# Rows of an image 34 words apart in place of 33

## What is computed

```
x = x + lattice(gn(x))        # 4 x 4 cells; each: concat of 1..3 inputs, 3x3 conv, bias, relu, 16..48 outputs
x = x + circular_conv(gn(x))  # 3x3, wraps around the edges (given as an FFT product)
x = x + spline_conv(gn(x))    # 3x3 over silu(x) and 8 cubic B-spline bases of x
x = x + conv(gn(x))           # 3x3, zero padding, bias
```

## Time and profile before

| | us |
|---|---|
| median of the runs | 1327.87 |
| lowest and highest of three | 1321.79, 1328.02 |
| span of the profiled execution, first to last instruction | 1313.7 |
| TensorE matmuls busy in it | 1177.5 |
| TensorE weight loads busy | 874.4 |
| VectorE busy | 772.7 |
| ScalarE busy | 701.6 |

### The profile page before, as it was taken

How to read it: one execution, slowest core, us unless ns; L and a number is a source line. 1 busy time by engine, 2 the same in 40 slices (tenths; PEclk the granted TensorE clock), 3 DMA queues, 4 the chain that set the end, 5 groups by cost and what they waited for, 6 DMA issues and landing times.

```text
span 1313.7 us, 14883 instructions
## 1 busy us (share of the span) xinstructions
PE 1177.5 (90%) x5088; PEld 874.4 (67%) x5088; DVE 772.7 (59%) x946; ACT 701.6 (53%) x740; POOL 380.5 (29%) x570
## 2 busy tenths in 40 slices
PE   1378998979999999999999999999998957999995
PEld 1255576756666677776666677777777745777774
DVE  6478983157555532235655553236656579889962
ACT  2456774254544444435454443333445499899931
POOL 7623333244531102122122213523034431102002
PEclk9989999989999999999999999999999978899997
DMA  7589998899999967889999987878789214676684
GB/s 98 148 210 236 258 269 226 203 196 205 211 209 187 215 175 200 226 185 193 219 205 181 206 235 190 244 199 218 188 206 170 45 25 68 100 117 102 108 127 62
DMA packets 108751, 232.12 MB, mean 177 GB/s; under 512 B 41332, under 2 KB 55236, under 8 KB 100484
## 3 DMA queue, kind: packets, MB, share of 16 engines
q1 hardware_dynamic: 91552, 205.02, 69.3%
q0 software_dynamic: 16576, 25.89, 10.6%
q10 hardware_dynamic: 548, 0.27, 0.2%
HBM read 122.05 MB, written 85.75 MB: 158 GB/s over the span
## 4 chain that ended last, share of the span: by engine, by line
PE 51%; SPq 17%; issue 7%; DVE 6%; ACT 6%; DMA 3%; POOL 1%; DVEq 0%; ACTq 0%; POOLq 0%
PE PB L1660 43%; SPq L762 13%; PE PB L1631 7%; SPq L745 4%; DMA lattice<-S 1%; DVE F L1486 1%; DVE S L1499 1%; ACT S L1184 1%; ACT F L1099 1%; PE PB L1622 1%; ACT F L1209 1%; DVE S L1493 1%; DMA S<-lattice 1%; ACT KAN L1082 1%; DMA F<-F 1%
## 5 line engine op out<-in xcount | busy, mean ns | idle before, releaser
L1660 PE MATMUL PB<-F,WA 128*96 128x512 f32 (+1 forms) x3792 | 920.9, 404 | 53.6 <-DVE F L1411 34.5
L1660 PEld LDWEIGHTS PB<-F,WA 128*96 128x96 f32 (+1 forms) x3792 | 664.7, 176 | 300.7 <-issue 52.3
L1099 ACT ACTIVATE F<-S 128x2116 fp32r<-128x2116 f32 (+4 forms) x160 | 261.4, 1635 | 228.5 <-issue 110.6
L1110 ACT ACTIVATE S<-PB,BIAS 96x512 f32<-96x512 f32 (+1 forms) x320 | 210.2, 680 | 276.0 <-PE PB L1660 275.8
L1399 DVE TENSOR_TENSOR F<-S,F 128x1089 fp32r<-128x1089 f32 (+2 forms) x80 | 121.4, 1518 | 198.9 <-ACT F L1099 198.6
L1411 DVE CAST F<-F 64x528 fp32r<-64x528 f32 (+4 forms) x304 | 190.7, 676 | 3.5
L1401 DVE TENSOR_TENSOR F<-S,F 128x1058 fp32r<-128x1058 f32 x64 | 80.7, 1261 | 183.1 <-ACT F L1099 182.5
L1631 PE MATMUL PB<-F,WA 128*128 128x512 f32 x576 | 150.7, 421 | 22.4 <-DVE F L1486 22.4
L854 POOL DMA_DIRECT2D WA<-taps x84 | 61.4, 735 | 350.4 <-ACT S L1110 335.7
L1631 PEld LDWEIGHTS PB<-F,WA 128*128 128x128 f32 x576 | 115.0, 201 | 52.6 <-issue 23.9
L1402 DVE TENSOR_TENSOR F<-S,F 64x1058 fp32r<-64x1058 f32 x64 | 79.9, 1248 | 0.0
(11 more groups left out here) (123 smaller groups left out, 746.8 us busy)
## 6 DMA issues: line engine op xcount, KB each, us to landing
lattice<-S SPq DMA_DIRECT2D x48, 817.5 KB, 6.0
S<-lattice SPq DMA_DIRECT2D x448, 66.1 KB, 4.7
lattice<-S SPq DMA_DIRECT2D x96, 272.5 KB, 3.9
S<-lattice SPq DMA_DIRECT2D x160, 136.1 KB, 2.9
S<-lattice SPq DMA_DIRECT2D x72, 272.5 KB, 4.9
S<-lattice SPq DMA_DIRECT2D x160, 70.1 KB, 2.9
S<-lattice SPq DMA_DIRECT2D x80, 136.2 KB, 4.6
S<-lattice SPq DMA_DIRECT2D x160, 66.0 KB, 2.8
```

The costliest lines, as they stand in the source:

```text
L1099: act.activation(piece_view(s, h, 0), raw_view(s, h), ACT.Copy).then_inc(hi_ready, 1)
L1110: act.activation(wide(to[:, at:at + TS])[:, :, 0:RX], pixels(RING_BANK[n % SLOTS_O][0:cell.rows, :]), ACT.Relu, bias=BIAS[0:cell.rows, k:k ...
L1660: last = nc.tensor.matmul(bank, WA[0:rows, first:first + cell.rows], wide(FZ[0:rows, i % SLOTS_F, base:base + TS])[:, :, 0:RX], start=j == ...
```

## The change

`RW` becomes `RX` + 2 = 34. With it `TS` is 544, `EVEN` 578, `PATCH` 1122, `SEG` 1123, `LEAD` 545, `PIECE` 2246 words. The longer buffers take more memory; the output buffer is cut into two tensors, and the one for odd images lies where the tap buffers RAW and RAW_ONE lay, now parts of one tensor TAPS_IN.

```diff
-RW = RX + 1
+RW = RX + 2
 TS = RQ * RW
...
-        RAW = [sb(f"RAW{i}", [NG * C, NG * C * 9]) for i in range(2)]
-        RAW_ONE = [sb(f"RAW_ONE{i}", [C, C * 9]) for i in range(2)]
+        TAPS_IN = sb("TAPS_IN", [4 * C, 2 * NG * C * 9 + 2 * C * 9])
+        RAW = [TAPS_IN[0:NG * C, i * NG * C * 9:(i + 1) * NG * C * 9] for i in range(2)]
+        RAW_ONE = [TAPS_IN[0:C, 2 * NG * C * 9 + i * C * 9:2 * NG * C * 9 + (i + 1) * C * 9] for i in range(2)]
         KAN = sb("KAN", [P, FEATS * K3, KC])
-        OT = sb("OT", [4 * C, 2, RQ, WD])
+        OT_NEW = sb("OT_NEW", [4 * C, RQ, WD])
+        OT = [OT_NEW[:, :, :], TAPS_IN[:, 0:RQ * WD].rearrange("p (y w) -> p y w", w=WD)]
...
-                yield out[b].rearrange("c (q r) w -> r c q w", r=4)[y], OT[y * C:(y + 1) * C, b % 2]
+                yield out[b].rearrange("c (q r) w -> r c q w", r=4)[y], OT[b % 2][y * C:(y + 1) * C]
...
-                        OT[:, b % 2].rearrange("p y (w s) -> p s y w", s=2)[:, s],
+                        OT[b % 2].rearrange("p y (w s) -> p s y w", s=2)[:, s],
```

## The result

The changed kernel takes 1346.47 us (median of four runs, 1342.11 to 1348.47), the kernel before 1327.94 beside it (1321.79 to 1332.1). The ratio of the two is 1.0171, with a 95% interval of 1.0135 to 1.0206: **slower by 1.7%**. The two medians lie 18.5 us apart, 1.4%, which is near the lower end of that interval; 1.71% of before would be 22.7 us. The time is outside the predicted range (1312 to 1337), on the side that had 0.17. The profiled execution took 1345.35 us, 1.85 more than its span of 1343.5.

What follows compares the result with a forecast made beforehand. It took TensorE's lattice matmuls to bound the middle and ScalarE the spline stage. Span 1313.7 - 4.8 (matmuls) + 3.5 (spline) + 2.0 (early transfers) = 1314.4 us, plus 14.2 outside the span: 1328.6 us, range 1312 to 1337.

Steps and rivals of the forecast that it cites:

- What bounds the kernel: Middle, 285 to 853 us: TensorE is busy throughout at full clock, so the lattice matmul's cost sets the time.
- That a matmul's fetch costs beyond its columns: Lattice matmuls at full clock: 24.4 ns of each 237.7 ns go to fetching the moving operand, not the array's columns.
- The price of a row: Lattice matmuls: 2.03 ns per row off a multiple of four words, so pitch 34 saves 4.8 us in all.
- The spline stage: Spline stage, going at ScalarE's pace: feature operations on 3% more words add 3.5 us (2 to 5).
- The part before 250 us: Start of the lattice, where SP has no slack: 3% more bytes in transfers add 2 us (0 to 4.5).
- Shared memory at nothing: Output buffer laid over the tap buffers: costs nothing, since the taps' last reader comes before its first write.
- Odd rows alone: Rival for matmul reads: only rows starting at odd words cost, 14.4 us saved, 1319.0 us; chance 0.30.
- even starts free: Rival for matmul reads: even starts lose their surplus, odd ones cost as now, about 1283 us; chance 0.10.
- The hop costs, whatever the start: Rival for matmul reads: they stay at 237.7 ns, longer operations add 5.5 us, 1333.4 us; chance 0.26.
- The base: Whole kernel: the profiled span of 1313.7 us lies 14.2 us below the median run, added to reach the forecast.

Runs made afterwards that it cites:

- experiment 4: Changed kernel with its large matmuls reading at pitch 32, all else at 34; 1324.82 us, ratio 0.9999. Its count: time over 0.24 us between starts over 0.3 us apart.
- experiments 5: TensorE alone, output zeros: 16 rows of 32 words, pitches 33 to 66, from words 0 to 3; pitch 41 from word 0 about 250 ns a matmul.
- experiment 9: TensorE alone, output zeros: 32 rows of 16 words, pitches 16 to 24, from words 0 to 3; pitch 20 from words 1 to 3 costs 40 to 43 ns over word 0.
- experiment 8: Changed kernel with all large matmuls reading at 33 and the spline's feature operations on 528 words; 1329.14 us, ratio 1.0059.
- experiment 7: Changed kernel with only the lattice's matmuls reading at 33, the spline's and last convolution's at 34; 1332.53 us, ratio 1.0084.
- experiment 2: Changed kernel with rows back at 33 words, keeping the shared memory; 1324.6 us against 1324.03, ratio 1.0013.
- experiments 1: TensorE alone, output zeros: 40 matmuls of each of 39 read patterns, twice; from word 0, pitch 33 takes 234.9 ns and 34 takes 246.8.

## Why the prediction was wrong

**What bounds the kernel: right.** TensorE fills the middle at the full clock, and the middle follows the matmul: 3088 matmuls of cells 5 to 15 by the 5.8 ns of the lattice's means are 17.9 us. The middle grew by 17.0 us from the one trace to the other; over all traces it is 776.7 us in the mean where the reads are at 33 and 790.7 at 34, 14 us. The rest is about what the waits get shorter: by the count of experiment 4 they come to 15.8 us in the mean at 33, and to 12.3 and 9.8 in the two traces at 34.

**That a matmul's fetch costs beyond its columns: right in kind, too large.** Of the 24.4 ns over 512 columns, contiguous rows from word 0, alone, keep 13.7 (227 against 213.3). At most some 10 ns come from the pitch of 33 and the starts; in the kernel, reading at 32 in place of 33 gives back 4.6.

**The step that failed is "The price of a row":** the 2.03 ns for "a row that is off a group of four words", each row counted by itself and priced by where it starts. By it pitch 34 was to save 2.9 ns in each matmul of kind "33", 4.8 us in all. The runs show the other sign. In the kernel, matmuls of every kind take more at 34, from any start: 5.8 ns in the mean (243.7 against 237.9). Alone, 33 takes 233.4 to 237.4 ns and 34 takes 240.0 to 246.8 over the four starts. And the kernel before with nothing but the lattice's reads at 34 is 1.24% slower. So 14 to 17 us were to be lost in the middle where 4.8 were to be gained. The mixture of starts in the trace before, which the prediction itself notes, couldn't show this.

Why a gap of two words is dearer than a gap of one word is argued and not shown. The account that comes nearest counts the groups of four over the whole matmul. At pitch 33 a row's last words and the next row's first can lie in one group, so that the 527 words from first to last are 132 groups (133 from words 2 and 3), not the 140 of the count by rows; at 34 the 542 words are 136 (137 from word 3), whether rows share groups, as from odd words, or not, as from even ones. The change then adds 3 to 4 groups from any start, which fits the alike starts, and 5.8 ns would be some 1.5 to 1.9 for each, near the 2.03 taken. But the patterns of experiments 5 and 9 that this count has wrong, and the length of the jump as a rival, leave it a guess.

The Trainium skill's "SBUF — State Buffer" (Specifications), with its penalty for each new 16-byte line, agrees in kind with the dearer reads of pitch 20 from words 1 to 3 (1.3 to 1.9 ns for each further group); the 42, 50 and 22 from odd words and the 66 differ from it, and the measurement decides. The even-word rule of the Trainium skill's "Vector Engine (DVE) Microarchitecture Reference" (§5.2) didn't carry over: at pitch 34, starts at 0, 1, 2 and 3 cost the same within 2 ns in the kernel.

**The spline stage: right.** The three kernels with 528-word tiles and experiment 8 take 223.3 to 225.4 us from the spline on (mean 224.8), the four with 544 words 227.9 to 229.6 (mean 228.7): 3.9 us for the predicted 3.5. By the stage's time, experiment 8 shows that the feature operations are its cause, experiment 7 that the matmuls aren't.

**The part before 250 us: right place, under-sized.** Cells 0 to 4 take 212.8 to 214.9 us with 33-word data (mean 213.8) and 217.0 to 219.7 with 34 (mean 218.3), whatever the matmuls read at: 4.5 us, where 2 were taken and 4.5 was the upper bound. The DMA share of the stretch is 0.99 (0.97 in the earlier trace rows), and SP's groups of five, now

```profile
124.52 6.07 SPq L764 DMA_DIRECT2D S<-lattice  x5
...
154.91 4.63 SPq L764 DMA_DIRECT2D S<-lattice  x5
160.25 4.93 SPq L764 DMA_DIRECT2D S<-lattice  x5
```

take 5.03 us in the mean of the seven between 100 and 165 us, where the eight before took 4.94: 1.7% more, no more than the bytes grew. Bytes fit, but no run parted them from the longer splits and from images that begin at odd words, so the cause is argued. The first matmul starts 3 us later on average with 34-word data (55.9 to 60.3 against 54.0 to 56.2); that overlaps, and stays open.

**Shared memory at nothing: right** (experiment 2).

**The rivals.** Odd rows alone, and even starts free, needed a difference by start that isn't there. "The hop costs, whatever the start" ended nearest, on the slower side, and its longer operations are in the result, with 8.4 us (4.5 and 3.9) for its 5.5; but it left matmuls at 237.7 ns, and they went to 244.

**The base.** Of the 14.2 us added between span and median about 1.8 lie around the span; the rest was that the execution profiled was faster than the four runs beside it. This shifts no sign.

## What to carry to other kernels

Padding that looks better aligned can be dearer: here rows 34 words apart cost more than rows 33 apart, from every start. Where a trace holds only one mixture of patterns, as this one did, a loop of matmuls alone prices the pitch, and is worth more than a share worked out of the mixture. Price the very shape that the kernel reads: the count of groups over the whole matmul had the sign right for 16 rows of 32 words, but with eight rows of 64 a gap of one word was no cheaper than two, and other pitches broke the count. And a bound taken away shows the next one: at pitch 32 the matmul lost 4.6 ns, and waits took back most of it.

## What was not expected of the hardware

Contiguous rows from word 0, alone and at the full clock, start 227 ns apart and not 213; the runs don't say why. One contiguous row of 512 words costs 9.7 ns more from word 1 than from word 0, for a single further group; from word 3, with the same further group, it is 2 ns (pitch 16 of experiment 9, 228.9). A gap of one whole group costs about 6 ns a matmul, whether there are 15 gaps (pitch 36 from word 0, 233.5; 236.7 in experiment 9) or 3 (four rows of 128 words, 132 apart, 233.3), but 13 to 16 with 31 gaps (pitch 20 from word 0, 240.1 and 243.3). And the same gap is far dearer off a group's start (36 from word 1: 256.4; 20 from word 1: 286.2), but for 42 and 22 it makes no difference. And the means come in steps: 94 of the 129 of experiments 1, 5 and 9 lie within 0.35 ns of a whole multiple of 3.33 ns (233.3, 246.7, 263.3, 296.7), the time of eight columns at 213.3 ns for 512, where chance would put a fifth there. No single count that was tried gives all of these; the full law stays open.
